# Scaling the gate inputs of a forgetting-style attention once per event instead of once per tile

## Chip, cores and metric

The kernel runs on one core of a Trainium2 chip. The metric is the device time of one execution in microseconds (us), lower is better. The kernel before took 2271.55 us (median of three runs, 2269.65 to 2274.39).

## What is computed

Input is x of 4 x 1024 tokens with 128 features, 4096 tokens in all. Four layers follow one another, each with a residual sum and a layer norm: an attention with 16 heads of 8, a mixture of 8 experts, an attention with 16 heads of 64 whose bias is gated, and a gated feed-forward block. The change lies where the third layer's operands are made:

```
q = rmsnorm((x @ Wq).reshape(B, T, 16, 64), q_rms_w)
k = rmsnorm((x @ Wk).reshape(B, T, 16, 64), k_rms_w)
v = (x @ Wv).reshape(B, T, 16, 64)
gate_logits = einsum('bthd,hd->bht', k, u_n) / 8
gate = softplus(gate_logits)
bias = -dist * omega_eff * gate
```

The gate logit of a token and head is linear in the key before its norm, so the kernel computes it from x with a 128 x 16 matrix G and multiplies it by the key's inverse root mean square afterwards.

## The kernel before

The program has three parts: the first attention, a middle part (the experts and everything up to the second attention's operands), and the second attention with the last feed-forward block. The change is in the last stage of the middle part. It works on 32 tiles of 128 tokens, four tiles to a chunk (`TILES`), eight chunks (`steps`). Each tile has three items, Q, K and V, so item n is tile n // 3 and kind n % 3 (`kinds`). Every engine has its own written-out loop over n; the engines meet only at semaphores.

- TensorE (`tensor_last`): `multiply(n)` (L2187) projects the tile into one of three pairs of PSUM banks. Before item n it waits until item n - 3 has left its pair (semaphore `scaled` for Q and K). Between the projections it transposes the scaled Q and K of three items ago (L2133), in jobs whose order is the list `line`, and once a chunk it transposes x (L2146) and multiplies it by G (L2152) for the gate inputs of the next chunk.
- ScalarE (`scalar_last`): squares Q and K (L2377), takes the root of the mean square (L2383), copies V (L2391), copies the transposed Q and K back with their weights (L2403), and copies the gate inputs to `z` (L2369).
- VectorE (`vector_last`): `reduce(n)` sums the squares of each head (L2239); one item later `scale(n)` takes the reciprocal (L2246), for K items multiplies the tile's 16 gate inputs in `z` by it (L2254), and multiplies Q or K by it out of PSUM (L2255). In each chunk it also builds the next x: `join` (sum of expert outputs L2211, statistics L2216 and L2219) after the K item of the chunk's first tile, and `norm` (L2224, L2230) after the K item of its second.
- GpSimd (`gpsimd_last`): for each tile, once K is transposed, `part` splits it into a high half (L2105) and a low half (L2107), and once a chunk it gathers expert outputs.
- The DMA queue of SyncE stores Q, V and both halves of K, two MB a tile, and from item 33 to item 53 also loads the first operands of the next stage.

The gates themselves are computed in three events, at items 24, 72 and 96 (`EVENTS`), for 2, 4 and 2 chunks at once. `gates_a` takes the absolute value of z (L2270), ScalarE applies Exp and Ln (L2409, L2411), `gates_b` does the rest (L2284 to L2292) and the result is transposed (L2156).

Of the kernel before, what the change touches and what calls it, by code (L numbers as in the profile page):

```python
# [16 lines left out]
P = 128  # L17
BANK = 512
CHUNK = 512
TILES = CHUNK // P  # L20
# [21 lines left out]
def sbuf(nc, ctx, name, shape, dt=F32):  # L42
    return ctx.enter_context(nc.sbuf_tensor(name, shape, dt))
# [1400 lines left out]
def middle(nc, ps, const, ins, scr, y0, tokens, experts, hidden, heads, dim, seq):  # L1444

    FC, HD = hidden // P, heads * dim
    PAIRS, NTILE, steps = HD // P, tokens // P, tokens // CHUNK
    NT = NTILE + experts - 1
    RB, NX, NS = 3, 6, 4
    with ExitStack() as ctx:  # L1450
        own = lambda n, shape, dt=F32: sbuf(nc, ctx, f"m{n}", shape, dt)
# [8 lines left out]
        xe, h = [own(f"xe{r}", [P, P]) for r in range(2)], [own(f"h{r}", [P, FC, P]) for r in range(2)]  # L1460
# [31 lines left out]
        sq, ss = [own(f"sq{r}", [P, HD]) for r in range(2)], [own(f"ss{r}", [P, heads]) for r in range(2)]  # L1492
# [3 lines left out]
        EVENTS = {24: range(0, 2), 72: range(2, 6), 96: range(6, 8)}  # L1496
        wide = TILES * max(len(cs) for cs in EVENTS.values())
        zabs, g, gj = own("zabs", [P, wide, heads]), own("g", [P, wide, heads]), own("gj", [P, wide, heads])
        z = own("z", [P, steps, TILES, heads])
        aug, augT = own("aug", [P, wide, P // heads, heads], F32R), [own(f"augT{r}", [4 * heads, CHUNK]) for r in range(2)]  # L1500
        warm = own("warm", [P, 1])
        tmp = sq[0]
# [461 lines left out]
        t_full, xT_full, z_full, weighted, aug_kept = sem("t_full"), sem("xT_full"), sem("z_full"), sem("weighted"), sem("aug_kept")  # L1964
        product, squared, reduced, rooted3, scaled, v_full = sem("product"), sem("squared"), sem("reduced"), sem("rooted3"), sem("scaled"), sem("v_full")
        ss_full, z_scaled, gated, soft, aug_full = sem("ss_full"), sem("z_scaled"), sem("gated"), sem("soft"), sem("aug_full")
# [3 lines left out]
        WQ, WK, WV = 0, 1, 2  # L1970
# [5 lines left out]
        events = [EVENTS[n] for n in sorted(EVENTS)]  # L1976
# [222 lines left out]
        def pair(n):  # L2199
            return ps[:, 2 * (n % 3):2 * (n % 3) + 2, :].rearrange("p a n -> p (a n)")  # L2200

        def vector_last():

            dve = nc.vector
# [36 lines left out]
            def scale(n):  # L2241

                (tile, kind), i = kinds(n), nth(n)
                c, t = divmod(tile, TILES)
                dve.wait_ge(rooted3, i + 1)
                dve.reciprocal(ss[i % 2][:, :], ss[i % 2][:, :]).then_inc(ss_full, 1)  # L2246
                dve.wait_ge(ss_full, i + 1)
                if i >= 3:
                    a = n // 3 * 3 + kind
                    old = [m for m in range(n) if kinds(m)[1] != WV][-3]  # L2250
                    dve.wait_ge(t_full, at["half", old, 1] + 1)
                if kind == WK:
                    dve.wait_ge(z_full, c + 1)
                    dve.tensor_tensor(z[:, c, t, :], z[:, c, t, :], ss[i % 2][:, :], ALU.mult).then_inc(z_scaled, 1)  # L2254
                dve.tensor_tensor(qk[i % 3][:, :].rearrange("p (h d) -> p h d", d=dim), pair(n).rearrange("p (h d) -> p h d", d=dim),  # L2255
                                  ss[i % 2][:, :].unsqueeze(2).to_broadcast([P, heads, dim]), ALU.mult).then_inc(scaled, 1)

            def parts(k):

                cs = events[k]  # L2260
                n = len(cs) * TILES
                return n, z[:, cs[0]:cs[-1] + 1, :, :].rearrange("p c t h -> p (c t) h"), zabs[:, 0:n, :], g[:, 0:n, :], gj[:, 0:n, :]

            def gates_a(k):

                n, zs, za, _, _ = parts(k)
                dve.wait_ge(z_scaled, (events[k][-1] + 1) * TILES)
                if k > 0:
                    dve.wait_ge(gated, GSTEP * k)
                dve.scalar_tensor_tensor(za, zs, -1.0, zs, ALU.mult, ALU.max).then_inc(gated, 1)  # L2270
# [57 lines left out]
            for n in range(NI + TLAG):  # L2328
                if 1 <= n <= NI and kinds(n - 1)[1] != WV:
                    scale(n - 1)  # L2330
                if n < NI and kinds(n)[1] != WV:
                    reduce(n)
                c, o = divmod(n, 12)
                if o == 2 and c + 1 < steps:
                    join(c + 1)
                if o == 5 and c + 1 < steps:
                    norm(c + 1)
                if n in EVENTS:
                    gates_a(event_of[EVENTS[n][0]])
                if n in lower_at:  # L2340
                    lower(lower_at.index(n))
                if n == LAST:
                    first_maxima(range(NM // 2))
                for late in (2, 3):
                    if n - late in EVENTS and late == (3 if n - late + 5 < NI else 2):
                        gates_b(event_of[EVENTS[n - late][0]])
# [136 lines left out]
def build(nc, ins, result, B, S, upto=5):  # L2483
# [18 lines left out]
    with ExitStack() as ctx:  # L2502
        const = {n: sbuf(nc, ctx, f"c_{n}", s, d) for n, s, d in (
            ("ident", [P, P], F32), ("identb", [P, P], BF16), ("mask_ji_add", [P, P], BF16), ("mask_ij", [P, BANK], BF16),
            ("ones", [P, 1], F32))}
        const["pair0"] = FirstPair(nc, S, DIM1)
        front = ctx.enter_context(ExitStack())
        const["zero"] = sbuf(nc, front, "c_zero", [P, BANK])
        const.update({n: sbuf(nc, front, f"c_{n}", [P, 6, P], d) for n, d in (("halves_in", F32), ("halves", BF16))})
        const.update({n: sbuf(nc, front, f"c_{n}", [P, P]) for n in ("mask", "mask_add")})  # L2510
        const.update({n: nc.alloc_semaphore(n) for n in ("id_in", "c_in", "c_set", "c_cast")})

        const["early"], const["zeroed"], const["n_zeroed"] = [], nc.alloc_semaphore("zeroed"), ZROWS // ZSTEP

        const["xs_shape"] = [P, ZSTEP // BANK, BANK]
        const["xs_part"] = lambda k: scr["xs"][k * ZSTEP:(k + 1) * ZSTEP, :].rearrange("(p a) d -> p (a d)", p=P).rearrange("p (r n) -> p r n", n=BANK)

        with front:
            y0 = sbuf(nc, front, "y0", [P, tokens // P, P])
            attention0(nc, ps, const, ins, scr, y0, B, H0, D0, S)  # L2520
            middle(nc, ps, const, ins, scr, y0, tokens, 8, 512, H1, DIM1, S)

        if upto >= 4:
            attend_and_finish(nc, ps, const, ins, scr, result, B, S, H1, DIM1, 512)
# [68 lines left out]
```

## Time and profile before

| | |
|---|---|
| median of three runs | 2271.55 us |
| the profiled execution's own time | 2270.39 us |
| its span, first to last instruction | 2268.6 us |
| TensorE busy over the span | 2053.4 us (91%) |
| VectorE busy over the span | 1373.6 us (61%) |
| ScalarE / GpSimd busy | 1157.6 / 843.4 us |
| mean granted TensorE clock | 0.955 |

The stage of the change runs from about 745 to 1064 us of the span. Busy time of TensorE is not work at its peak, since matmuls are pipelined. A row of a group gives line, engine, operation, output and inputs, shapes and count; then busy time in us and mean ns of one; then the idle time of the engine just before the group's instructions and what ended it. A row of the timeline gives start in us, length in us, engine, line, operation and count, and in brackets the idle time before it and its releaser.

### The profile page before, as it was taken

To read this page: it belongs to the slowest core of one execution; us is meant where nothing else is said; L and a number is where in the kernel's file an instruction comes from. 1 tells how busy PE (TensorE), PEld (TensorE's weight loads), DVE (VectorE), ACT (ScalarE), POOL (GpSimd) and SP (SyncE) were. 2 spreads that over 40 slices of the span, in tenths; PEclk is the share of its full clock that TensorE was granted. 3 is DMA by queue.
4 is the path that set the end of the run, shared out by engine and by line. 5 is a ranking of instruction groups with operands and counts; after the bars stand their busy time and mean duration, and the time that the engine had idled before them with its cause. 6 is when DMAs were issued, how large, how long until landed. Compare 5 with 4: busy or idle time off the path is not lost.

```text
span 2268.6 us, 34364 instructions
## 1 busy us (share of the span) xinstructions
PE 2053.4 (91%) x11728; PEld 1167.7 (51%) x11728; DVE 1373.6 (61%) x3345; ACT 1157.6 (51%) x1859; POOL 843.4 (37%) x544
## 2 busy tenths in 40 slices
PE   5799999998487879886899999999999999999998
PEld 2333333334476445444566556655666556655644
DVE  4777777774732678875566666666667655333311
ACT  2366666667343667674455555555555543223232
POOL 5000000000601445432577777777777773000000
PEclk8899999999589899996899999999999999999999
DMA  5233333111365579977667766776677677543300
GB/s 178 96 128 129 127 114 127 57 51 59 103 184 146 171 221 323 282 221 203 148 160 178 180 162 157 179 180 164 154 180 179 167 208 186 136 98 84 89 5 10
DMA packets 263468, 335.88 MB, mean 148 GB/s; under 512 B 22828, under 2 KB 185948, under 8 KB 262888
## 3 DMA queue, kind: packets, MB, share of 16 engines
q1 hardware_dynamic: 247992, 305.82, 50.2%
q0 software_dynamic: 7664, 24.39, 3.0%
q10 hardware_dynamic: 7640, 3.48, 0.5%
q8 instruction: 95, 1.56, 0.3%
q14 instruction: 77, 0.63, 0.1%
HBM read 193.69 MB, written 122.62 MB: 139 GB/s over the span
## 4 chain that ended last, share of the span: by engine, by line
PE 42%; issue 6%; DVE 4%; DMA 1%; SPq 0%; ACT 0%; DVEq 0%; ACTq 0%
PE ps L1284 10%; PE ps L953 7%; PE ps L937 6%; PE ps L906 6%; PE ps L938 6%; PE ps L1235 3%; DVE a1mx L1009 2%; PE ps L940 1%; PE ps L1295 1%; PE ps L1272 1%; PE ps L1273 1%; DVE a1mx L1005 1%; DMA a1FQ<-s_q 1%; DVE a1mx L1002 0%; PE ps L909 0%
## 5 line engine op out<-in xcount | busy, mean ns | idle before, releaser
L1120 POOL TENSOR_TENSOR a1sum<-a1sum,a1prob 128x1024 f32<-128x1024 f32 (+3 forms) x256 | 463.8, 1812 | 84.0 <-ACT a1prob L1063 51.2
L1063 ACT ACTIVATE a1prob<-ps 128x512 f32<-128x512 f32 (+2 forms) x640 | 328.0, 553 | 245.8 <-PE ps L940 214.5
L476 DVE TENSOR_REDUCE a0grid<-ps 128x8 f32<-128x1024 f32 x288 | 346.9, 1221 | 116.5 <-PE ps L351 71.9
L1002 DVE CUSTOM_DVE_ANT_0 ps<-ps,c_mask_ij 128x128 f32<-128x128 f32 x496 | 264.4, 551 | 194.3 <-issue 190.0
L577 ACT ACTIVATE a0prob<-ps 128x1024 f32<-128x1024 f32 x288 | 292.6, 1025 | 171.6 <-PE ps L377 91.5
L937 PE MATMUL ps<-a1QA,a1KA 69*128 69x512 f32 (+3 forms) x768 | 285.6, 379 | 5.0 <-DMA a1QA<-a1neg 5.0
L953 PE MATMUL ps<-a1prob,a1V 128*64 128x512 f32 (+3 forms) x1536 | 273.8, 499 | 5.0 <-ACT a1prob L1063 5.0
L938 PE MATMUL ps<-a1QB,a1KB 128*128 128x512 f32 (+3 forms) x768 | 264.3, 352 | 0.0
L906 PE MATMUL ps<-a1KA,a1QA 68*128 68x128 f32 x744 | 225.0, 381 | 4.6 <-DMA a1KA<-s_g 3.8
L953 PEld LDWEIGHTS ps<-a1prob,a1V 128*64 128x64 f32 x1536 | 102.9, 138 | 173.3 <-issue 138.7
L1005 DVE TENSOR_REDUCE a1mx<-ps 128x1 f32<-128x320 f32 x248 | 146.0, 589 | 70.5 <-PE ps L906 67.6
L937 PEld LDWEIGHTS ps<-a1QA,a1KA 69*128 69x128 f32 x768 | 149.7, 195 | 49.8 <-issue 42.2
L398 PE MATMUL ps<-a0prob,a0V 128*32 128x512 f32 (+3 forms) x1536 | 163.6, 499 | 1.3 <-ACT a0oT L584 1.3
L938 PEld LDWEIGHTS ps<-a1QB,a1KB 128*128 128x128 f32 x768 | 149.2, 194 | 7.6
L1117 POOL TENSOR_TENSOR a1sum<-a1prob 128x768 f32<-128x768 f32 x64 | 135.1, 2111 | 44.7 <-ACT a1prob L1063 44.7
L906 PEld LDWEIGHTS ps<-a1KA,a1QA 68*128 68x128 f32 x744 | 134.8, 195 | 29.2 <-DVE a1mx L1005 6.1
L270 POOL DMA_DIRECT2D s_xs<-c_zero x19 | 13.6, 715 | 331.4 <-DVE y L503 331.4
L351 PE MATMUL ps<-a0BK,a0Q 51*128 51x512 f32 x512 | 130.5, 507 | 5.8 <-DMA a0BK<-s_k 5.0
L1284 PE MATMUL ps<-fhb,fh 128*128 128x512 f32 x256 | 111.2, 593 | 0.0
L1284 PE MATMUL ps<-fhc,fh 128*128 128x512 f32 x256 | 111.2, 592 | 0.0
L351 PEld LDWEIGHTS ps<-a0BK,a0Q 51*128 51x128 f32 x512 | 49.2, 189 | 110.0 <-issue 90.5
L377 PE MATMUL ps<-a0BQ,a0K 51*128 51x512 f32 x384 | 89.9, 465 | 16.2 <-DVE a0grid L476 12.0
(267 smaller groups left out, 3196.1 us busy)
## 6 DMA issues: line engine op xcount, KB each, us to landing
a1FQ<-s_q SPq DMA_DIRECT2D x128, 256.0 KB, 7.9
a1KB<-s_k SPq DMA_DIRECT2D x128, 256.0 KB, 8.5
s_xs<-c_zero POOLq DMA_DIRECT2D x19, 1024.0 KB, 8.9
s_q<-mqkT SPq DMA_DIRECT2D x32, 512.0 KB, 3.4
s_v<-mv SPq DMA_DIRECT2D x32, 512.0 KB, 5.8
s_k<-a1KH SPq DMA_DIRECT2D x32, 512.0 KB, 5.0
s_k<-a1KL SPq DMA_DIRECT2D x32, 512.0 KB, 6.0
a1KA<-s_k SPq DMA_DIRECT2D x64, 256.0 KB
```

Source lines behind the costliest of these rows:

```text
L351: end = pe.matmul(half(x, m), Q[g % 2][r:r + ROWS, t * P:(t + 1) * P], BK[g % 2][r:r + ROWS, :, j * P:(j + 2) * P], start=True, stop=t != j2)
L476: dve.tensor_reduce(grid[g % 2][:, :, a:b + 1:b - a], banks(("max", k)), axis=AX.X, op=ALU.max).then_inc(s1_free, 1)
L577: act.activation(prob[:, :, a:b + 1:b - a, :], banks(("exp", q)), ACT.Exp).then_inc(p_full, 1)
L906: last = pe.matmul(bank[:, 0:j1 - j0], QA[b][0:ROW, h, t * P:(t + 1) * P], KA[b][0:ROW, h, j0:j1], start=True, stop=True)
L937: pe.matmul(s, KA[b][0:ROW + 1, h, keys], QA[b][0:ROW + 1, h, queries], start=k == 0, stop=False)
L938: last = pe.matmul(s, KB[b][:, h, keys], QB[b][:, h, queries], start=False, stop=not diag)
L953: last = pe.matmul(O[h * dim:(h + 1) * dim, off:BANK], V[b][:, j, h * dim:(h + 1) * dim], p[:, h, off:BANK], start=j == 0, stop=u == LAST[c])
L1002: dve.tensor_tensor_reduce(bank[:, 0:w], bank[:, 0:w], const["mask_ij"][:, BANK - w:BANK], 1.0, LOWEST, ALU.add, ALU.max, mx[:, x % 2, h, ...
L1005: dve.tensor_reduce(mx2[:, x % 2, h, t - IT // 2:t - IT // 2 + 1], bank[:, 0:w], axis=AX.X, op=ALU.max).then_inc(job_free, 1)
L1063: act.activation(weights_of(g, u)[:, group[0]:group[-1] + 1, off:BANK], both(e, u, group), ACT.Exp).then_inc(weighed, 1)
L1120: pool.tensor_tensor(t[:, :, off:BANK], t[:, :, off:BANK], weights_of(g, u)[:, :, off:BANK], ALU.add).then_inc(summed, 1)
L1284: end = pe.matmul(b, w[:, k, o * P:(o + 1) * P], source[:, k, :], start=k == 0, stop=k == FC - 1)
```

## The change

The reciprocal of a K item is written to a new buffer `kss`, which keeps the norms of all 32 tiles, and both the scaling of K and the gates read it there. The 32 multiplications of 128 x 16 gate inputs are gone; `gates_a` does one multiplication over all tiles of its event, of 128 x 128, 128 x 256 and 128 x 128, ahead of the absolute value, and waits for the gate inputs and the norms of the event's last chunk and then for its own product. Line numbers from there on move by a line or two: the reciprocal is L2248, the scaling L2254, the new product L2269.

```diff
-        z = own("z", [P, steps, TILES, heads])
+
+        z, kss = own("z", [P, steps, TILES, heads]), own("kss", [P, steps, TILES, heads])
...
                 dve.wait_ge(rooted3, i + 1)
-                dve.reciprocal(ss[i % 2][:, :], ss[i % 2][:, :]).then_inc(ss_full, 1)
+                norms = kss[:, c, t, :] if kind == WK else ss[i % 2][:, :]
+                dve.reciprocal(norms, ss[i % 2][:, :]).then_inc(ss_full, 1)
                 dve.wait_ge(ss_full, i + 1)
...
-                if kind == WK:
-                    dve.wait_ge(z_full, c + 1)
-                    dve.tensor_tensor(z[:, c, t, :], z[:, c, t, :], ss[i % 2][:, :], ALU.mult).then_inc(z_scaled, 1)
                 dve.tensor_tensor(qk[i % 3][:, :].rearrange("p (h d) -> p h d", d=dim), pair(n).rearrange("p (h d) -> p h d", d=dim),
-                                  ss[i % 2][:, :].unsqueeze(2).to_broadcast([P, heads, dim]), ALU.mult).then_inc(scaled, 1)
+                                  norms.unsqueeze(2).to_broadcast([P, heads, dim]), ALU.mult).then_inc(scaled, 1)
...
                 n, zs, za, _, _ = parts(k)
-                dve.wait_ge(z_scaled, (events[k][-1] + 1) * TILES)
+                cs = events[k]
+                dve.wait_ge(z_full, cs[-1] + 1)
+                dve.wait_ge(ss_full, 2 * TILES * (cs[-1] + 1))
+                dve.tensor_tensor(zs, zs, kss[:, cs[0]:cs[-1] + 1, :, :].rearrange("p c t h -> p (c t) h"), ALU.mult).then_inc(z_scaled, 1)
+                dve.wait_ge(z_scaled, k + 1)
```

On VectorE, the K item of a chunk's first tile and the `join` behind it stood so before (`mss` the norms, `mz` the gate inputs, `mqk` the scaled Q or K, `macc` the joined x):

```order
L2246 RECIPROCAL mss1<-mss1 128x16
L2254 TENSOR_TENSOR mz<-mz,mss1 128x16
L2255 TENSOR_TENSOR mqk0<-ps,mss1 128x1024
L2211 SCALAR_TENSOR_TENSOR macc0<-mx1,myg0 128x512
L2216 BN_STATS mst2<-macc0 128x6 x4
L2219 BN_AGGR mmv2<-mst2 128x2 x4
L2239 TENSOR_REDUCE mss0<-msq0 128x16
```

and stand so now:

```order
L2248 RECIPROCAL mkss<-mss1 128x16
L2254 TENSOR_TENSOR mqk0<-ps,mkss 128x1024
L2212 SCALAR_TENSOR_TENSOR macc0<-mx1,myg0 128x512
L2217 BN_STATS mst2<-macc0 128x6 x4
L2220 BN_AGGR mmv2<-mst2 128x2 x4
L2240 TENSOR_REDUCE mss0<-msq0 128x16
```

The small product between reciprocal and scaling is gone, and the sum of `join` stands directly behind the scaling. At the first event, item 24, VectorE now has:

```order
L2240 TENSOR_REDUCE mss0<-msq0 128x16
L2269 TENSOR_TENSOR mz<-mz,mkss 128x128
L2273 SCALAR_TENSOR_TENSOR mzabs<-mz 128x128
L2248 RECIPROCAL mss0<-mss0 128x16
L2254 TENSOR_TENSOR mqk1<-ps,mss0 128x1024
```

The one product of the event stands between the item's reduction and the absolute value. The order on the other engines is unchanged.

## Rows read from the trace of the kernel before

**Rows 1.** Groups of instructions on VectorE, 745 to 1045 us
```profile
L2255 DVE TENSOR_TENSOR mqk<-ps,mss 128x1024 f32<-128x1024 f32 x64 | 78.0, 1219 | 1.1
L2239 DVE TENSOR_REDUCE mss<-msq 128x16 f32<-128x1024 f32 x64 | 77.4, 1209 | 28.4 <-ACT msq L2377 28.0
L2254 DVE TENSOR_TENSOR mz<-mz,mss 128x16 f32<-128x16 f32 x32 | 35.4, 1108 | 1.1
L2230 DVE TENSOR_SCALAR mxout<-macc,mmv,mrs 128x128 f32<-128x128 f32 x28 | 7.8, 343 | 0.3
```
**Rows 2.** Small product, sum of `join`: min/median/max ns, first and last start
```profile
L2254 DVE TENSOR_TENSOR mz<-mz,mss x32: 174/370/2310, 750.9 to 1033.7; 128x16 f32<-128x16 f32 x32
...
L2211 DVE SCALAR_TENSOR_TENSOR macc<-mx,myg x8: 674/686/1731, 733.8 to 978.8; 128x512 f32<-128x512 f32 x8
```
**Rows 3.** Timeline of VectorE around two K items
```profile
784.59 0.17 DVE L2254 TENSOR_TENSOR mz<-mz,mss 128x16 f32<-128x16 f32 x1
...
785.82 1.73 DVE L2211 SCALAR_TENSOR_TENSOR macc<-mx,myg 128x512 f32<-128x512 f32 x1
...
793.64 2.30 DVE L2254 TENSOR_TENSOR mz<-mz,mss 128x16 f32<-128x16 f32 x1
795.87 1.21 DVE L2255 TENSOR_TENSOR mqk<-ps,mss 128x1024 f32<-128x1024 f32 x1
...
797.20 1.12 DVE L2230 TENSOR_SCALAR mxout<-macc,mmv,mrs 128x128 f32<-128x128 f32 x4
```
**Rows 4.** Timeline of GpSimd around the same two
```profile
784.59 2.41 POOL L2107 TENSOR_TENSOR a1KL<-mqkT,a1KH 128x1024 fp32r<-128x1024 f32 x1
...
793.56 2.36 POOL L2107 TENSOR_TENSOR a1KL<-mqkT,a1KH 128x1024 fp32r<-128x1024 f32 x1
```
**Rows 5.** Groups of instructions on TensorE, 745 to 1045 us
```profile
L2187 PE MATMUL ps<-mwk,mflip 128*128 128x512 f32 x128 | 68.5, 662 | 23.2 <-DVE mqk L2255 23.2
L2187 PE MATMUL ps<-mwq,mflip 128*128 128x512 f32 x124 | 62.8, 631 | 12.9 <-DVE mqk L2255 12.9
```
**Rows 6.** Timeline of TensorE, projections of K that waited
```profile
762.38 3.68 PE L2187 MATMUL ps<-mwk,mflip 128*128 128x512 f32 x4 [2.37 <-DVE mqk L2255]
...
797.14 1.98 PE L2187 MATMUL ps<-mwk,mflip 128*128 128x512 f32 x4 [2.37 <-DVE mqk L2255]
...
874.68 3.46 PE L2187 MATMUL ps<-mwk,mflip 128*128 128x512 f32 x4 [2.36 <-DVE mqk L2255]
...
998.97 1.99 PE L2187 MATMUL ps<-mwk,mflip 128*128 128x512 f32 x4 [1.23 <-DVE mqk L2255]
```
**Rows 7.** Timeline of TensorE around the first event's second half
```profile
836.08 1.98 PE L2187 MATMUL ps<-mwq,mflip 128*128 128x512 f32 x4 [0.88 <-DVE mqk L2255]
```
**Rows 8.** A stretch: busy PE, PEld, DVE, ACT, POOL (instructions); clock, DMA share, GB/s
```profile
862.00:935.00 73.00, 64.26 (x254) 35.57 (x253) 62.24 (x88) 51.02 (x82) 36.18 (x26) 0.95 1.07 326
```
**Rows 9.** Waits, 745 to 1045 us: total us, times, longest
```profile
POOL a1KH L2105 <- DMA s_k<-a1KL: 7.6, 1, 7.6
...
ACT mv L2391 <- DMA s_v<-mv: 4.8, 4, 1.7
```
**Rows 10.** Gate products of the events, groups on VectorE
```profile
L2285 DVE TENSOR_TENSOR mg<-mg,mom 128x256 f32<-128x256 f32 x1 | 0.4, 426 | 0.0
...
L2285 DVE TENSOR_TENSOR mg<-mg,mom 128x128 f32<-128x128 f32 x1 | 0.3, 292 | 0.0
```
**Rows 11.** Timeline at the first event
```profile
817.72 0.28 DVE L2270 SCALAR_TENSOR_TENSOR mzabs<-mz 128x128 f32<-128x128 f32 x1
...
817.73 1.28 ACT L2409 ACT_TABLE_LOAD   x1
```
**Rows 12.** Timeline at the last event
```profile
1034.90 1.31 DVE L2270 SCALAR_TENSOR_TENSOR mzabs<-mz 128x128 f32<-128x128 f32 x1
...
1036.73 0.31 ACT L2409 ACTIVATE mzabs<-mzabs 128x128 f32<-128x128 f32 x1
```
**Rows 13.** Timeline of TensorE, the next stage's first product
```profile
1065.00 0.77 PE L937 MATMUL ps<-a1QA,a1KA 69*128 69x512 f32 x1 [2.36 <-DMA a1QA<-a1neg]
```

## The prediction

> **What bounds the kernel now.** I read first the groups of the stage, then the small product's own line, then the timelines of VectorE and GpSimd side by side, and last TensorE's waits. The groups on VectorE show the reader something odd: the product of 128 x 16 gate inputs, whose input is a sixty-fourth of the scaling's, costs 1108 ns on average, 35.4 us in all [rows 1]. Its own line spreads from 174 to 2310 ns [rows 2], so it isn't work but waiting. The timelines say on what. At 784.59 the product starts together with GpSimd's split of K and takes 0.17 us; at 793.64 it starts 0.08 us after that split, takes 2.30 us, and the scaling of K starts only 2.23 us after the product did, when the split of 2.36 us is over [rows 3, 4]. Counted along the timeline, 13 of the 32 products take 2.29 to 2.31 us, six 0.37, one 0.50, one 0.89 and eleven 0.17 or 0.18, which adds up to the 35.4 us. Products and sums that read two operands in SBUF wait for GpSimd; the scaling, which takes one from PSUM, never does (mean 1219 ns [rows 1], though it often lies beside the split).
>
> TensorE is what the end hangs on: it waits for the K scaling before each projection of K, 23.2 us in all, and for the Q scaling 12.9 us [rows 5]. The waits before K come in 14 places: one of 0.24 us, and thirteen that stand one by one behind the thirteen long products: 2.37, 2.37, 1.70, 0.83, 1.24, 2.36, 2.36, 1.53, 2.19, 2.36, 1.71, 0.66 and 1.23 us, 22.9 together, the first and the last in [rows 6]. So a product that looks off the path sits on it thirteen times. The next stage starts once this one is through, at 1065.00 [rows 13], and all that follows shifts with it.
>
> **Term 1, the products removed.** Each long one gives TensorE at most 2.2 us (the 2.23 above) and no more than it waited. Five waits reach 2.36 or more: 5 x 2.2 = 11.1. Six others are worth what they lasted: 1.70 + 1.24 + 1.53 + 2.19 + 1.71 + 1.23 = 9.6. The remaining two (0.83 and 0.66) stand behind the products at 825.90 and 975.40, where VectorE then runs without idle through `join` and `gates_b`, so that TensorE waits again, at 836.08 for 0.88 us [rows 7]; there the whole shift counts, less 1.05 us that `join` will now lose (term 3): 2 x 1.15 = 2.3. Sum 23.0. The nineteen short products had no wait behind them: 0.
>
> **Term 2, the slow projections.** Four of the thirteen waits are followed by a projection of four instructions that takes 3.46 to 3.68 us, the others by one of 1.98 [rows 6]; the granted clock of these stretches is below 1, as 0.95 in [rows 8], so part of the time is at 1.2 GHz instead of 2.4. Together they cost 6.4 us above 1.98 each. The same idle of 2.37 us was also followed by 1.98, so it is not certain that the idle did it: between 0 and 6.4. They lie behind the longest idles, which go, and VectorE hides little; I take 5.
>
> **Term 3, the wait that moves.** GpSimd's split is still there, and the next instruction with two operands in SBUF meets it. That is the sum of `join`: 1.73 us at 785.82, beside the split [rows 3], against a median of 0.69 [rows 2]: some 1.05 more. After three long products (825.90, 934.51, 975.40) `join` follows at once; two are in term 1, the third costs 1 us. Then `norm`: its four L2230 follow the product in the chunk's second tile, five times a long one. No row shows one beside the split, since the product always took the wait (mean 343 ns [rows 1]). If they block as the sum does, each time about 0.95 us: the split of 793.56 ends at 795.92, and the four, at 797.20 now [rows 3, 4], would start 2.23 us earlier, at 794.97. Between 0 and 4.7; they delay only the next reduction, so I take 1.5.
>
> For these the trace has no row, but the Trainium skill does: "SBUF — State Buffer", section Who interferes with whom, lets a DVE instruction with two SBUF inputs wait for a GpSimd one that reads SBUF, as the trace shows here with 2.30 us, and lets tensor_scalar and cast contend too where they run in a two-port mode. By that rule `norm` pays the whole 4.7 us and the sum below would be 17.3 instead of 20.5.
>
> **Term 4, the stores.** From 862 to 935 us the DMA engines are busy all the time, share 1.07 at 326 GB/s [rows 8]. ScalarE waits there four times for the store of V two tiles back, 4.8 us, and GpSimd once for 7.6 us [rows 9]. A faster stage can't draw these bytes faster, and ScalarE's wait, now under the long product, comes into view. The gain of this stretch from the two long products at 871.20 and 905.95 is 2 x 2.2 plus two of the slow projections, about 7.5. Between 0 and 11 can be lost (all four waits of the stretch with their slow projections); I take 5, between half and all of the 7.5.
>
> The Trainium skill would see more room: "SBUF — State Buffer", section Summary: rules for kernel authors, plans with about 358 GB/s between HBM and SBUF. The 23.8 MB of this stretch would then take 66.5 us, not 73, and nothing of term 4 would be lost: the sum would be 25.5. The trace's stretch, with its engines busy throughout, reached 326, and the sum goes by that.
>
> **Term 5, what is added.** Three products, 0.29, 0.43 and 0.29 us by the nearest operation of the same shapes [rows 10], each up to 2.3 us if it meets the split. They stand ahead of the absolute value that ScalarE's Exp needs, and VectorE is queued behind them with the next reciprocal. At the first event ScalarE loads a table from 817.73 for 1.28 us while VectorE is done at 818.00 [rows 11], so 1 us is covered; the second is alike. At the last the absolute value already waits for the split, ends at 1036.21, and Exp starts at 1036.73 [rows 12]: the new product takes over that wait, and 0.29 more fits into the 0.52. So 0; uncovered they cost 1 us, blocked outside the cover at most 4. The reciprocal with another output and the scaling with another input keep shape and memory: 0.
>
> **Sum.** 23.0 + 5 - 1 - 1.5 - 5 = 20.5 us. The profiled execution took 2270.39, so 2249.9; it lies 1.2 us below the median of the runs, so the forecast is 2271.55 - 20.5 = 2251 us.
>
> **Rivals.**
> - *All pays out.* The products delay the scalings by 13 x 2.2 plus 4 for the short ones, 33 us, and if that slack also eats the 12.9 us of waits before Q, the gain is 33: 2238. For it: nothing is lost by taking work out of a chain. Against it: 19 products had no wait behind them. Chance 0.13.
> - *The stores hold it.* Nothing is gained from 862 to 935, which takes another 5 us, and the backlog eats the next two waits (2.2 and 1.7): gain 11.5, 2260. For it: share 1.07. Against: ScalarE waited only four times, 1.7 us at the longest [rows 9]. Chance 0.15.
> - *The wait only changes its name.* VectorE is idle 28.0 us before its reductions already [rows 1]; if TensorE then waits as long for the Q scaling or the transposes, nothing changes: 2271. Against it: the thirteen waits stand exactly behind the thirteen long products. Chance 0.07.
> - *Slower.* GpSimd's wait of 7.6 us for the store of K's low half [rows 9] is hidden now. If the denser stores make such waits pass to the copies of K and through them to TensorE, each costs up to 7.6 us; from the third on (22.8) the 20.5 are gone, and with a fourth it is 2281. It needs stores to land later than two tiles. Chance 0.05.
> - My forecast, gain 15 to 28, has 0.60.
>
> **The numbers.** The likeliest case gives 2251, by itself 2243 to 2257. The range takes in the stores' case above and most of the payout below: 2237 to 2264, about 0.86 of the chance. A measurement here tells 0.2% (4.5 us) from no change. Faster by more: 0.60 + 0.15 + 0.13 = 0.88; same 0.07; slower 0.05.
>
> **What would show it.** The K group on TensorE waits under 4 us instead of 23.2; three L2269 of 0.3 to 0.5 us or one with a wait for the split; more sums of `join` near 1.7 us; L2231 above 343 ns if `norm` blocks; ScalarE's wait for the store of V above 4.8 us; L937 first at about 1044, and the same distance from there to the end. The prediction is wrong if the waits before Q grow beyond 12.9 us by what those before K lose, or if the part after L937 changes its length.

## The result and the profile after

The changed kernel took 2256.32 us (median of four runs, 2253.90 to 2257.49) beside 2272.97 us for the kernel before (four runs, 2269.65 to 2275.03): 16.6 us less, ratio 0.9927, 95% interval 0.9906 to 0.9948, which is a gain of 12 to 21 us. The profiled execution took 2257.29 us, its span is 2255.5.

The groups of instructions on VectorE, 745 to 1030 us, answer to [rows 1]:

```profile
L2254 DVE TENSOR_TENSOR mqk<-ps,mkss 128x1024 f32<-128x1024 f32 x32 | 39.2, 1225 | 1.3 <-DVE mkss L2248 0.2
...
L2231 DVE TENSOR_SCALAR mxout<-macc,mmv,mrs 128x128 f32<-128x128 f32 x28 | 11.2, 458 | 0.3
L2212 DVE SCALAR_TENSOR_TENSOR macc<-mx,myg 128x512 f32<-128x512 f32 x7 | 11.1, 1581 | 0.0
```

The 35.4 us of small products are gone. The sum of `join` went from 7.9 to 11.1 us and the last step of `norm` from 7.8 to 11.2: both took over a part of the wait. The groups on TensorE answer to [rows 5]:

```profile
L2134 PE MATMUL ps<-c_ident,mqk 128*128 128x128 f32 x512 | 69.6, 277 | 8.5 <-ACT mflip L2367 5.7 <-DVE mqk L2254 1.3 <-ACT maugT L2421 0.9
L2188 PE MATMUL ps<-mwk,mflip 128*128 128x512 f32 x128 | 62.9, 615 | 1.1 <-DVE mqk L2254 1.1
L2188 PE MATMUL ps<-mwq,mflip 128*128 128x512 f32 x125 | 61.8, 616 | 14.5 <-DVE mqk L2254 14.5
```

The wait before K fell from 23.2 to 1.1 us, that before Q rose from 12.9 to 14.5, and the one behind ScalarE's copy of the transposed x (`mflip`) grew from 0.4 to 5.7. The projections of K took 615 ns each instead of 662, 6 us together: three of the four slow ones are gone, one of 3.33 us remains at 872.69, behind one of the waits for `mflip`. The line of the three products of the events, with min/median/max in ns:

```profile
L2269 DVE TENSOR_TENSOR mz<-mz,mkss x3: 280/415/1356, 809.6 to 1015.0; 128x128 f32<-128x128 f32 x2, 128x256 f32<-128x256 f32 x1
```

and the timeline at the last event, which answers to [rows 12]:

```profile
1014.99 1.36 DVE L2269 TENSOR_TENSOR mz<-mz,mkss 128x128 f32<-128x128 f32 x1
...
1016.38 0.29 DVE L2273 SCALAR_TENSOR_TENSOR mzabs<-mz 128x128 f32<-128x128 f32 x1
1016.91 0.31 ACT L2412 ACTIVATE mzabs<-mzabs 128x128 f32<-128x128 f32 x1
```

The last product met the split and waited for it in place of the absolute value, which ended at 1016.67, before ScalarE's table was loaded at 1016.89. The next stage's first product on TensorE came at 1045.17, by the timeline, against 1065.00 before [rows 13]:

```profile
1045.17 0.77 PE L937 MATMUL ps<-a1QA,a1KA 69*128 69x512 f32 x1 [2.35 <-DMA a1QA<-a1neg]
```

The next stage thus starts 19.8 us earlier in this execution, but the span is only 13.1 shorter: 6.7 us were lost behind that product. The windows of 20 us that begin 20 us behind it, before (from 1085.00) and after (from 1065.20), with busy PE, PEld, DVE, ACT and POOL, granted clock, DMA share and GB/s, show where:

```profile
1085.00:1105.00 20.00, 18.36 (x81) 11.00 (x77) 11.95 (x54) 7.46 (x14) 14.64 (x8) 0.93 0.54 130
```

```profile
1065.20:1085.20 20.00, 20.00 (x57) 11.68 (x53) 7.89 (x35) 5.98 (x10) 10.50 (x6) 0.53 0.55 133
```

TensorE ran 81 products in the one and 57 in the other, at a mean granted clock of 0.93 and 0.53. By the clock's records, in the kernel before the stretch at the 1.2 GHz level around the next stage's start lasted 47.8 us, in this execution 64.9.

### The profile page after: what moved, and what is told of

It reads as the page before. It is cut to its first block, busy times and chain, and to the rows that moved or that the text cites. A ratio compares the mean times of both kernels' runs of the same rounds, so it can differ in the third digit from the quotient of the medians.

```text
span 2255.5 us, 34337 instructions
## 1 busy us (share of the span) xinstructions
PE 2055.8 (91%) x11728; PEld 1170.4 (52%) x11728; DVE 1351.2 (60%) x3316; ACT 1158.0 (51%) x1859; POOL 844.3 (37%) x544
## 4 chain that ended last, share of the span: by engine, by line
PE 43%; issue 6%; DVE 3%; DMA 1%; SPq 0%; ACT 0%; DVEq 0%; ACTq 0%
PE ps L1284 10%; PE ps L953 7%; PE ps L937 6%; PE ps L906 6%; PE ps L938 6%; PE ps L1235 3%; DVE a1mx L1009 2%; PE ps L940 1%; PE ps L1295 1%; PE ps L1272 1%; PE ps L1273 1%; DVE a1mx L1005 1%; DMA a1FQ<-s_q 1%; DVE a1mx L1002 0%; PE ps L909 0%
## 5 line engine op out<-in xcount | busy, mean ns | idle before, releaser
L937 PE MATMUL ps<-a1QA,a1KA 69*128 69x512 f32 (+3 forms) x768 | 287.4, 382 | 4.8 <-DMA a1QA<-a1neg 4.8
L937 PEld LDWEIGHTS ps<-a1QA,a1KA 69*128 69x128 f32 x768 | 150.7, 196 | 49.8 <-issue 42.0
L377 PE MATMUL ps<-a0BQ,a0K 51*128 51x512 f32 x384 | 89.9, 465 | 16.3 <-DVE a0grid L476 12.2
```

The lines of the kernel that those rows point to most:

```text
L937: pe.matmul(s, KA[b][0:ROW + 1, h, keys], QA[b][0:ROW + 1, h, queries], start=k == 0, stop=False)
```

## The experiments

Times are medians, ratios are to runs of the kernel before on the same chip. The first product L937 alone is no clean measure of the stage, since the stage doesn't begin at the same moment in every execution: before it the kernels do the same work, and yet ScalarE's copy of the first tile's V starts at 746.7 to 755.5 us. So the stage's length is taken here from the start of that copy to the first L937; all of them are in the table further down. In the kernel before and in the changed one the copy is:

```profile
750.47 1.00 ACT L2391 ACTIVATE mv<-ps 128x1024 f32<-128x1024 f32 x1
```

```profile
750.77 1.01 ACT L2394 ACTIVATE mv<-ps 128x1024 f32<-128x1024 f32 x1
```

That is 314.5 and 294.4 us of stage.

**One input instead of two.** To separate the wait for GpSimd from the cost of having an instruction there:

```diff
-                    dve.tensor_tensor(z[:, c, t, :], z[:, c, t, :], ss[i % 2][:, :], ALU.mult).then_inc(z_scaled, 1)
+                    dve.reciprocal(z[:, c, t, :], ss[i % 2][:, :]).then_inc(z_scaled, 1)
```

> The kernel before, with the small product of each K tile replaced by a reciprocal of the same 128 x 16 elements with one input in SBUF (the gate inputs are overwritten by the root mean square instead of being multiplied, so the gates are not those of the reference). Same number of instructions, same places, same waits for semaphores. Theory, the product waits for GpSimd's split because it reads two operands in SBUF: each replacement takes about 0.25 us and never 2.3, the waits of TensorE before K fall from 23 us to under 4, and the time is that of the changed kernel within 4 us, about 2256 to 2260. Rival, an instruction at that place costs by its being there or by its wait for the gate inputs: 2.3 us stay in some of them and the time stays at 2272.

Measured: 2253.70 us, ratio 0.9928 (0.9907 to 0.9949), the same as the changed kernel. The line's own view shows the replacement 32 times at one and the same length:

```profile
L2254 DVE RECIPROCAL mz<-mss x32: 252/253/254, 751.9 to 1016.1; 128x16 f32<-128x16 f32 x32
```

TensorE's wait for the scalings of K and Q was 15.6 us, as after the change, and the stage took 295.9 us, against 293.9 to 295.2 in four profiles of the changed kernel. So an instruction in the same place, with the same waits for semaphores, costs 1 to 2 us of stage at most, and nothing that the times show; what cost time was the blocking of the product. Operation and second operand were changed together, so this run alone doesn't say which of the two lets the instruction pass. The Trainium skill ("SBUF — State Buffer", section Who interferes with whom) says that a DVE instruction with at most one SBUF input outside the two-port modes does not contend with GpSimd; the 252 to 254 ns agree.

**The product behind the scaling.** To separate VectorE's busy time from what is queued behind it:

```diff
-                if kind == WK:
-                    dve.wait_ge(z_full, c + 1)
-                    dve.tensor_tensor(z[:, c, t, :], z[:, c, t, :], ss[i % 2][:, :], ALU.mult).then_inc(z_scaled, 1)
                 dve.tensor_tensor(qk[i % 3][:, :].rearrange("p (h d) -> p h d", d=dim), pair(n).rearrange("p (h d) -> p h d", d=dim),
                                   ss[i % 2][:, :].unsqueeze(2).to_broadcast([P, heads, dim]), ALU.mult).then_inc(scaled, 1)
+                if kind == WK:
+                    dve.wait_ge(z_full, c + 1)
+                    dve.tensor_tensor(z[:, c, t, :], z[:, c, t, :], ss[i % 2][:, :], ALU.mult).then_inc(z_scaled, 1)
```

> The kernel before, with the small product of each K tile behind the scaling of K instead of ahead of it; nothing else. Theory, what cost time was that the scaling, and TensorE behind it, stood in the queue behind the blocked product: the product still waits for the split where they meet, now about 1.1 us instead of 2.3 since the scaling passes first, TensorE's waits before K fall under 4 us, and the time is 2255 to 2262. Rival, it is VectorE's busy time that counts: it falls only from 35 to about 20 us in this line and a good half of the gain is missing, 2264 or more.

Measured: 2256.70 us, ratio 0.9944 (0.9922 to 0.9965). The groups on VectorE, 745 to 1030 us:

```profile
L2256 DVE TENSOR_TENSOR mz<-mz,mss 128x16 f32<-128x16 f32 x32 | 34.5, 1079 | 0.0
...
L2230 DVE TENSOR_SCALAR mxout<-macc,mmv,mrs 128x128 f32<-128x128 f32 x28 | 7.8, 342 | 0.3
...
L2211 DVE SCALAR_TENSOR_TENSOR macc<-mx,myg 128x512 f32<-128x512 f32 x7 | 4.8, 680 | 0.0
```

and the projections of K on TensorE:

```profile
L2187 PE MATMUL ps<-mwk,mflip 128*128 128x512 f32 x128 | 62.7, 613 | 1.0 <-DVE mqk L2252 0.9
```

The theory's numbers came: the median product takes 1172 ns, the waits before K are 1.0 us, and the time lies in its range. What failed is the rival's premise that VectorE's time in this line falls to some 20 us: the products still cost 34.5, since they wait less each time (1862 ns at the longest) but more often. So most of the gain needs no busy time saved: what cost it was that the scaling, and TensorE behind it, stood in the queue behind a blocked instruction. It is not the whole gain, though. The stage took 299.8 us, 12 to 15 us less than before, but some 5 more than the changed kernel's 293.9 to 295.2, and its median is 4.2 us above that of the changed kernel on the same chip (2252.52, below), though there the intervals overlap. Through what the last 5 us pass is not shown. With the product behind the scaling, `join` and `norm` run at their free lengths (680 and 342 ns), since the product takes the wait for them, as before.

**Both kernels again.** Nothing edited:

> The kernel before once more, as a control: 2272. Its profile shows whether the stretch at the 1.2 GHz level that begins some 16 us ahead of the next stage's first product has the same length in another execution (about 48 us) or varies; if it varies, the 6.7 us that the changed kernel's profile loses between 20 and 43 us after that product are not a property of the change.

> The changed kernel once more, as a control: 2256. If the longer stretch at 1.2 GHz (about 65 us instead of 48) belongs to the change, this profile has it too and the distance from the next stage's first product to the end is 6.7 us longer than in the kernel before; if it is chance, it may be gone, and then the time of this execution is near 2250.

Measured: the kernel before 2270.88 us, ratio 1.001 (0.9994 to 1.0026); the changed one 2252.52 us, ratio 0.993 (0.9908 to 0.9951). The changed kernel's second profile had the long stretch again (64.9 us, against 51.2 in the second profile of the kernel before). Two more profiles of it, since two may be chance:

> The changed kernel a third time, for its profile alone. Two profiles of it show a stretch at the 1.2 GHz level of 64.9 us around the next stage's first product, and 1210 us from that product to the end; the eight other profiles of this study show 47.8 to 54.6 us, and seven of them 1203 to 1204.5 us. If the long stretch belongs to the change, it is here again; if two executions of the same kernel can differ in it, this one or the next may show 48 to 55 us and 1203 to 1205 us to the end.

> The changed kernel a fourth time, for its profile alone; expected as in the third.

Measured: 2250.69 and 2254.76 us, one execution each (the kernel before on this chip: 2267.44). The two differ. Their windows that begin 20 us behind the first product of the next stage, the third profile, then the fourth:

```profile
1063.80:1083.80 20.00, 18.39 (x79) 10.37 (x75) 10.94 (x48) 8.25 (x16) 14.36 (x9) 0.91 0.51 128
```

```profile
1063.20:1083.20 20.00, 20.00 (x59) 11.97 (x55) 7.89 (x35) 5.72 (x10) 10.24 (x6) 0.55 0.52 130
```

All profiles of the two kernels and, for the sections around this one, of the experiments: the start of the first copy of V, the first L937 of the timeline, the stage's length between them, the span from L937 to the end, and the length of the stretch at 1.2 GHz in the clock's records:

| kernel | first copy of V | first L937 | stage | to the end | stretch |
|---|---|---|---|---|---|
| before | 750.47 | 1065.00 | 314.5 | 1203.6 | 47.8 |
| before, second | 752.28 | 1064.09 | 311.8 | 1204.5 | 51.2 |
| changed | 750.77 | 1045.17 | 294.4 | 1210.3 | 64.9 |
| changed, second | 746.71 | 1041.60 | 294.9 | 1210.0 | 64.9 |
| changed, third | 748.65 | 1043.82 | 295.2 | 1205.1 | 51.2 |
| changed, fourth | 749.35 | 1043.23 | 293.9 | 1209.8 | 64.9 |
| one input | 751.52 | 1047.41 | 295.9 | 1204.5 | 51.2 |
| product behind | 751.06 | 1050.83 | 299.8 | 1204.1 | 51.2 |
| delay | 751.17 | 1053.18 | 302.0 | 1203.0 | 54.6 |
| half the delay | 750.09 | 1048.02 | 297.9 | 1213.1 | 68.3 |
| third buffer for V | 755.53 | 1041.52 | 286.0 | 1208.4 | 51.2 |
| join later | 751.51 | 1053.18 | 301.7 | 1203.4 | 47.8 |
| both | 754.29 | 1052.05 | 297.8 | 1203.6 | 47.8 |

The same program can have either length of the stretch. Averaged, the changed kernel's next stage begins 21.1 us earlier (1043.5 against 1064.5) and gives 4.8 us back behind it (1208.8 against 1204.0): 16.3 us, beside the measured gain of 16.6. Of the 21.1 us, 18.6 lie in the stage (294.6 against 313.2) and 2.5 ahead of it, where nothing was changed.

**A delay ahead of the next stage.** If the stretch's length hangs on when the next stage starts, a delay should shorten it:

```diff
                 dve.wait_ge(pair0.max_done, NM)
+                for r in range(2):
+                    dve.tensor_reduce(ss[r][:, :], aug[:, :, :, :].bitcast(F32).rearrange("p t a h -> p (t a h)").rearrange("p (h d) -> p h d", h=heads), axis=AX.X, op=ALU.add)
                 upper = mx[:, 0, :, IT // 2:IT]
```

> The changed kernel with two reductions of 128 x 2048 added on VectorE between the last maximum and the row of maxima (their results are not used), which delays the next stage's first product by 4.4 us. In both profiles of the changed kernel a stretch at the 1.2 GHz level, which begins ahead of that product, lasted 64.9 us, in both of the kernel before 47.8 and 51.2, and the part behind the product took 6 us longer. Theory, where that stretch ends hangs on when the first products come relative to it, so that a small shift of the stage can lengthen it or shorten it: with the delay it falls to about 51 us as in the two earlier experiments, whose first products came 2 to 6 us later, and the total rises by less than 1 us. Rival, the longer stretch belongs to what the change does: it stays near 65 us and the total rises by 4.4 us.

Measured: 2258.03 us, ratio 0.9938 (0.9916 to 0.996); first L937 at 1053.18, stretch 54.6 us, 1203.0 us to the end. The stretch and the part behind the product spoke for the theory. The total stood between theory and rival: by the ratios it rose by some 2 us, not by under 1 and not by 4.4, and its interval contains both. So half the delay (`range(1)`) followed:

> The changed kernel with one reduction of 128 x 2048 added before the row of maxima, half the delay of the experiment before: 2.2 us. That one brought the stretch at 1.2 GHz to 54.6 us and the total to 0.9938 of the kernel before, where the changed kernel had 0.9927 and 0.993. Theory, as there: the stretch is 48 to 55 us and the part behind the first product 1203 to 1205 us, so the total is that of the changed kernel within 1.5 us though 2.2 us were added. Rival: the stretch stays at 65 us and the total rises by 2.2 us.

Measured: 2255.78 us, ratio 0.9944 (0.9928 to 0.9961). The profiled execution was the slowest of its five (2262.93): stretch 68.3 us, 1213.1 us to the end. Part of the latter is another stretch of 6.8 us at 1.2 GHz, late in this execution (at 1840 in the clock's records), which of all the others only the third buffer's profile below has too. The theory falls as a rule: a delay of 2.2 us did not shorten the stretch in this execution. One profile for each delay says no more, since profiles of one and the same kernel differ as much. What decides between some 50 and some 65 us is open.

**A third buffer for V.** For term 4, the stores:

```diff
-                if tile > 1:
-                    act.wait_ge(v_out[tile % 2], 16 * (tile // 2))
-                act.activation(v[tile % 2][:, :], pair(n), ACT.Copy).then_inc(v_full, 1)
+                if tile > 2:
+                    act.wait_ge(v_out[tile % 3], 16 * (tile // 3))
+                act.activation(v[tile % 3][:, :], pair(n), ACT.Copy).then_inc(v_full, 1)
...
```

The lines left out lay the third buffer over the input buffers of x, which this stage doesn't use, give each buffer a semaphore for its store, and let the events' product report on another semaphore.

> The changed kernel with three buffers for V instead of two, so that ScalarE copies V without waiting for the store of two tiles back; nothing else moves (the third buffer lies in memory that the stage doesn't use). In the changed kernel's profile ScalarE waits 6.7 us for those stores and TensorE 5.7 us for the transposed x behind them. Theory, the stores hold part of the stage through this wait: ScalarE's wait goes, TensorE's 5.7 us go, and the next stage's first product comes 4 to 6 us earlier. Rival, the stretch is bound by the bytes: the wait passes to the stores of K, through GpSimd's split, and the first product comes within 1.5 us of where it was.

Measured: 2245.61 us (2242.11 to 2251.68), ratio 0.9875 (0.985 to 0.99), the fastest version of all, some 12 us below the changed kernel by the ratios and outside its intervals. The waits of its stage, 745 to 1030 us, with their total, number and longest:

```profile
POOL a1KH L2111 <- DMA s_k<-a1KL: 32.0, 7, 7.9
...
PE ps L2193 <- DVE mqk L2259: 14.2, 14, 4.4
...
ACT mv L2399 <- DMA s_v<-mv: 2.4, 2, 1.8
```

against the same views of the changed kernel:

```profile
PE ps L2188 <- DVE mqk L2254: 15.6, 17, 3.7
...
POOL a1KH L2106 <- DMA s_k<-a1KL: 12.4, 2, 6.6
...
ACT mv L2394 <- DMA s_v<-mv: 6.7, 5, 2.7
```

TensorE's 5.7 us for `mflip` don't appear any more. The stores still have a backlog, but it now stands at GpSimd (32.0 us instead of 12.4), which TensorE doesn't need so soon. From 862 to 935 us, the changed kernel and this one:

```profile
862.00:935.00 73.00, 64.19 (x260) 35.63 (x259) 57.63 (x83) 51.79 (x83) 36.70 (x25) 0.98 1.05 325
```

```profile
862.00:935.00 73.00, 69.20 (x284) 38.85 (x285) 60.79 (x93) 57.77 (x94) 39.47 (x28) 1.00 1.08 332
```

The DMA engines move the bytes at nearly the same rate in both, and as in the kernel before (326), but TensorE is busy 5 us longer in the same 73. The stage took 286.0 us, 8.6 less than the changed kernel's average: more than the 4 to 6 expected. So the rival, by which the bytes hold the stage's length, is out, though its other half, the wait that passes to the stores of K, came. That the first L937 comes at 1041.52, only 2 us before the changed kernel's average, has another reason: the stage began at 755.53, 6.7 us later than there. The version with both edits, which also has three buffers, begins at 754.29, all others between 746.71 and 752.28; whether the third buffer delays the work ahead of the stage is open. The profiled execution was also the slowest of the five (2251.68) and has, like that of half the delay, a late stretch of 6.8 us at 1.2 GHz. So 8.6 of the 12 us are shown in the stage by one profile, the rest isn't.

**Join and norm one item later.** For term 3, the wait that moved:

```diff
-                if o == 2 and c + 1 < steps:
+                if o == 3 and c + 1 < steps:
                     join(c + 1)
-                if o == 5 and c + 1 < steps:
+                if o == 6 and c + 1 < steps:
                     norm(c + 1)
...
-                if o == 3 and c + 1 < steps:
+                if o == 4 and c + 1 < steps:
                     root2(c + 1)
```

> The changed kernel with the join and the norm of the next chunk's x one item later on VectorE, behind the reduction of Q instead of directly behind the scaling of K, and the root for it one item later on ScalarE. Theory, the wait for GpSimd's split has moved from the product to the join (7 of them, mean 1581 ns against 680 free) and the norm (mean 458 ns against 343, 28 of them): behind the reduction the split is over, both means fall to the free values, TensorE's five waits of about 1.1 us before the Q that follows shrink, and the next stage begins 4 to 8 us earlier. Rival, these waits are hidden or the stores bound the stage: the busy time falls by the same 9 us, but the first product comes within 1.5 us of where it was.

Measured: 2260.66 us, ratio 0.9958 (0.9941 to 0.9974), slower than the changed kernel by 6 to 7 us, though the intervals still touch; the stage took 301.7 us, 7.1 more. Neither theory foresaw this. The groups on VectorE and TensorE, 745 to 1030 us:

```profile
L2231 DVE TENSOR_SCALAR mxout<-macc,mmv,mrs 128x128 f32<-128x128 f32 x28 | 7.8, 342 | 0.3
L2212 DVE SCALAR_TENSOR_TENSOR macc<-mx,myg 128x512 f32<-128x512 f32 x7 | 4.8, 688 | 0.0
L2294 DVE TENSOR_TENSOR maug<-mg,maug 128x128 fp32r<-128x128 f32 (+1 forms) x2 | 3.7, 1868 | 0.1
```

```profile
L2188 PE MATMUL ps<-mwq,mflip 128*128 128x512 f32 x126 | 68.4, 669 | 11.8 <-DVE mqk L2254 10.3 <-issue 1.5
...
L2157 PE MATMUL ps<-c_ident,maug 128*128 128x128 f32 x24 | 4.2, 301 | 7.9 <-DVEq L2296 7.9
```

The moved wait is gone (both means free), and TensorE waits less before Q, 11.8 us for 14.5. But `join` now stands directly ahead of `gates_b` in the items of two events, and meeting the split has moved once more, to the last products of `gates_b`: the two L2294 took 3.7 us, 0.7 in the changed kernel. The transposes of the gates behind them wait 7.9 us instead of 2.8; the projections of Q took 669 ns instead of 616, 6.7 us together. So this experiment shows that the wait can be moved, not what it was worth.

**Both of the last two.**

> The changed kernel with both: three buffers for V, join and norm one item later. If the two waits are independent, the gains add up, 8 to 14 us in the stage; if the stores bound the stage, it is no better than the better one of the two by more than 2 us.

Measured: 2258.31 us, ratio 0.9936 (0.9914 to 0.9957), stage 297.8 us. They don't add up: the later join costs more than the third buffer brings. That it is no better than the better one of the two is what the second expectation said for a stage bound by the stores; here it doesn't speak for that, since the later join by itself costs 7.1 us of stage.

## Why the prediction held

**The direction and the mechanism** held. The small product was a wait for GpSimd's split, taken ahead of an instruction that TensorE needs. The one-input experiment shows the first half, the swapped order most of the second. The forecast was 2251 us; 2256.32 lies in its likeliest band.

**Term 1, the products (23.0).** The waits before K fell from 23.2 to 1.1 us, as their total said. The second profile of the kernel before had only 20.6 us of them, so the sum started from an execution that had more to give.

**Term 2, the slow projections (5 of 6.4).** Three of the four went in the profiled execution and one stayed, though shorter; with the others a little shorter too it is 6 us by the group's mean. But slow projections come and go between executions: in the second profile of the kernel before the K projections had a mean of 640 ns, in the later ones of the changed kernel 598 to 620.

**Term 3, the moved wait (1.05 for a join, 1.5 for the norms).** `join` was blocked six times of seven instead of three, three times more as forecast. `norm` was blocked in five chunks, also as counted; the first of its four steps waits for the split of 790.67 to 793.03, by the timelines of VectorE and GpSimd:

```profile
792.09 1.79 DVE L2231 TENSOR_SCALAR mxout<-macc,mmv,mrs 128x128 f32<-128x128 f32 x4
```

```profile
790.67 2.36 POOL L2108 TENSOR_TENSOR a1KL<-mqkT,a1KH 128x1024 fp32r<-128x1024 f32 x1
```

The four took 1.79 us where they are 1.12 when free [rows 3]: 0.67 each time, 3.4 in all, between the 1.5 that I took and the 4.7 of the upper bound. Here the rule of the Trainium skill ("SBUF — State Buffer", section Who interferes with whom), that tensor_scalar can contend as well, was right where no row of the kernel before showed it. The sum with its price whole, 17.3, is as near to the 18.6 us that the stage gained as the forecast's 20.5, so that doesn't decide between them. How much of these 3.4 us reaches TensorE stays open, as the experiment meant for it lost elsewhere.

**Term 4, the stores (5).** Well sized, and by the mechanism given: ScalarE's wait for the store of V came out from under the product and grew from 4.8 to 6.7 us. It reached TensorE through the copy of the transposed x, which stands behind V's copy on ScalarE. The timeline of the changed kernel:

```profile
870.39 1.02 ACT L2394 ACTIVATE mv<-ps 128x1024 f32<-128x1024 f32 x1 [2.66 <-DMA s_v<-mv]
871.31 0.59 ACT L2367 ACTIVATE mflip<-ps 128x512 f32<-128x512 f32 x1
...
871.96 0.94 PE L2134 MATMUL ps<-c_ident,mqk 128*128 128x128 f32 x4 [2.88 <-ACT mflip L2367]
```

Twice this cost TensorE 2.8 to 2.9 us, 5.7 together (5.2, 5.0 and 2.6 in the other three profiles, 0.4 before). But what was lost was not lost to the bytes: the rate stayed at 325 to 332 GB/s in all three kernels, as the term had it, and still a third buffer took the wait away and shortened the stage by 8.6 us. The figure of 358 GB/s in the Trainium skill ("SBUF — State Buffer", section Summary: rules for kernel authors), by which nothing would be lost, was not reached in this stretch; the waits were waits for a buffer.

**Term 5, what is added (0).** Right: 0.28 and 0.41 us under ScalarE's loads of tables, and at the end 1.36 us in place of the absolute value's wait.

**The sum.** From the first copy of V to the first L937, TensorE's idle time fell from 53.7 to 40.4 us in the first pair of profiles and its busy time from 260.9 to 254.1: 13.3 and 6.8, where the forecast had 15.5 (23 less terms 3 and 4) and 5. That is 20.1 for 20.5. Over all profiles the stage gained 18.6. That the first pair comes out so exactly is partly luck: it has the longer stage of the two profiles of the kernel before.

**The size.** 20.5 us were forecast, 16.6 measured, and 20.5 still lies inside the interval of 12 to 21. Some 2 us are the terms. The rest is the sentence that all which follows shifts with the stage: on average 4.8 us came back behind it, in executions whose stretch at 1.2 GHz was longer, and 2.5 of them were covered by a stage that began earlier, which the prediction didn't have either. The prediction had named its own sign for this, that the part after L937 changes its length, and the sign came: 1210 instead of 1204 us in three of four profiles of the changed kernel and in neither of the two of the kernel before; of the seven other kernels one has a long stretch. Whether the change makes it more likely is open, and so is what triggers it.

## What to carry to other kernels

An instruction that takes far longer than its size explains, with a minimum of 174 ns and a maximum of 2310, is waiting; lay the other engines' timelines beside it. If it then stands ahead of something that the bounding engine needs, move it behind that or take it out: here moving it brought some 13 of the 18.6 us of stage, with its busy time nearly unchanged. A wait that is removed lets the next one show, so look in the trace for who stood behind the same lock and which store was hidden by it. Try each by itself: a third buffer for V brought two thirds as much again as the change, moving `join` by one item lost 6 to 7 us. And measure a stage from its own start to its end: the moment at which the next one begins also holds what varied ahead of it, up to 9 us here.

## What was unexpected of the hardware

- A tensor_scalar on VectorE (128 x 128 in float32, SBUF to SBUF) waits for a GpSimd operation as a product of two SBUF tensors does: 1026 ns at the longest for one of 338 ns.
- The stretch at the 1.2 GHz level around a pause of TensorE had 47.8 to 68.3 us in executions of nearly the same program, two lengths (51.2 and 64.9) even in executions of one and the same kernel. The long one cost some 5 us of 2255, as much as a measurement's interval reaches to either side here.
